# A graph kernel's attention weights written to PSUM as well, and its one-hots made by four scalar comparisons

## What is computed

```python
Q, K, V = x @ WQ, x @ WK, x @ WV             # per node, in 8 heads
Eh = edge_attr @ WE                          # per edge
score = exp(clip((K[src] * Q[dst] / sqrt(16) * Eh).sum(-1), -5, 5))   # per edge and head
wV = segment_sum(V[src] * score, dst)        # per node
Z = segment_sum(score, dst)
h = x + wV / (Z + 1e-6)                      # then a batch norm over the nodes
```

## Time and profile before

| | |
|---|---|
| timed runs | 5692.21, 5694.81, 5681.8 us; median 5692.21 |
| the profiled execution | span of 4693.0 us from its first to its last instruction; no other time of it is given |
| TensorE busy | 3812.3 us (81%) |
| VectorE busy | 3158.1 us (67%) |
| GpSimd busy | 3369.7 us (72%) |
| ScalarE busy | 1078.1 us (23%) |
| layer 0's loop over chunks | 145.7 to 2300.0 us |
| layer 0's gathers | 81.1 to 2286.1 us, 1661 of them |
| layer 1's gathers | 2443.8 to 4538.9 us, 1661 of them |

### The profile page before, as it was taken

The page is one execution under the profiler, slowest core; times in us unless marked ns, Lnnn a source line. Parts: engine busy times, 40 slices in busy tenths (PEclk is TensorE's granted clock), DMA queues, the critical chain, the costliest instruction groups (busy, mean ns, idle before and its releaser), DMA issues. The chain is left out here.

```text
span 4693.0 us, 76906 instructions
## 1 busy us (share of the span) xinstructions
PE 3812.3 (81%) x19332; PEld 3161.6 (67%) x19333; DVE 3158.1 (67%) x8279; ACT 1078.1 (23%) x4010; POOL 3369.7 (72%) x3437
## 2 busy tenths in 40 slices
PE   6889899989989988888898977777777777777778
PEld 5777777777778877767567755655555556555555
DVE  1877677677777776777646866666666666666657
ACT  3100010000000000000034433333333333333324
POOL 3677777777777777777557777777777777777752
PEclk9887787787776787888687555555555555555559
DMA  7666665666666666666424322222222222222224
GB/s 279 182 182 184 176 189 176 179 183 181 183 181 182 182 183 174 185 179 183 148 86 97 61 61 61 61 61 61 61 61 61 61 61 60 60 61 61 61 58 154
DMA packets 376029, 593.47 MB, mean 126 GB/s; under 512 B 151298, under 2 KB 204520, under 8 KB 374488
## 3 DMA queue, kind: packets, MB, share of 16 engines
q0 software_dynamic: 132880, 330.18, 27.4%
q1 hardware_dynamic: 241544, 255.24, 18.2%
q10 hardware_dynamic: 1552, 7.43, 0.4%
HBM read 551.16 MB, written 40.54 MB: 126 GB/s over the span
## 5 line engine op out<-in xcount | busy, mean ns | idle before, releaser
L393 POOL DMA_INDIRECT kv_g<-kv_table,idx x1661 | 1678.2, 1010 | 568.0 <-issue 498.7
L1065 POOL DMA_INDIRECT xg<-xl_table,idx x1661 | 1583.0, 953 | 519.3 <-issue 498.6
L1130 PEld LDWEIGHTS ps_sum<-pw,xg 128*128 128x128 f32 x3328 | 740.9, 328 | 165.9 <-DVE pws L1271 165.5
L1130 PE MATMUL ps_sum<-pw,xg 128*128 128x64 f32 x3328 | 819.1, 428 | 4.7 <-DVE pws L1271 2.2
L452 PE MATMUL ps_sum<-kv_g,hot 128*64 128x136 f32 x3328 | 606.6, 339 | 246.8 <-issue 245.8
L1117 PE MATMUL ps_tops<-ident,top 128*64 128x128 f32 x832 | 285.9, 447 | 518.7 <-DVE top L1243 518.4
L452 PEld LDWEIGHTS ps_sum<-kv_g,hot 128*64 128x64 f32 x3328 | 480.9, 167 | 314.9 <-issue 310.2
L438 PE MATMUL ps_pair<-w,eat 128*128 128x128 f32 x3328 | 616.3, 342 | 5.1 <-issue 5.1
L438 PEld LDWEIGHTS ps_pair<-w,eat 128*128 128x128 f32 x3328 | 524.2, 240 | 109.3 <-issue 71.7
L442 PE MATMUL ps_pair<-qw,hott 64*128 64x128 f32 x3328 | 583.9, 326 | 2.9 <-DMA qw<-q_table 2.9
L1229 DVE SCALAR_TENSOR_TENSOR ps_lg<-raw 128x256 f32<-128x256 f32 x416 | 185.3, 445 | 573.4 <-ACT raw L1178 566.7
(11 more groups left out here) (160 smaller groups left out, 4684.9 us busy)
## 6 DMA issues: line engine op xcount, KB each, us to landing
eat<-in_edges SPq DMA_DIRECT2D x416, 256.0 KB
local<-local_table SPq DMA_DIRECT2D x416, 128.0 KB, 3.8
kv_g<-kv_table,idx POOLq DMA_INDIRECT x1661
xg<-xl_table,idx POOLq DMA_INDIRECT x1661
qw<-q_table SPq DMA_DIRECT2D x416, 32.0 KB
adw<-ad_row SPq DMA_DIRECT2D x416, 32.0 KB, 5.1
kv_table<-kv_out SPq DMA_DIRECT2D x25, 512.0 KB, 2.6
xl_table<-xl SPq DMA_DIRECT2D x25, 264.0 KB, 2.8
```

The costliest lines, as they stand in the source:

```text
L393: nc.gpsimd.indirect_dma_start(out=kv[:, u, k, 0:2 * D], out_offset=None, in_=m["kv_table"], in_offset=bass.IndirectOffsetOnAxis(ap=idx[:, ...
L1065: nc.gpsimd.indirect_dma_start(out=xg[:, u, k], out_offset=None, in_=m["xl_table"], in_offset=bass.IndirectOffsetOnAxis(ap=idx[:, u // B, ...
L1130: nc.tensor.matmul(ps_sum[:, b, 0:W], xg[:, u, k, 0:D], pw[:, b, k], start=(k == 0), stop=(k == K - 1))
```

## The change

The PSUM bank that held the numbers 0 to 63 now holds the attention weights. ScalarE computes Exp of the scores twice, once into `kv_g` as before and once into this bank, and raises the semaphore `weighed` with the second. `value` reads the weights from the bank. `one_hot` no longer has the copy of the numbers in PSUM; it makes the one-hot slot by slot, with four `tensor_scalar` instructions that compare `m["iota"]` in SBUF (128 x 64) with one node number per partition. The copy of the numbers to PSUM ahead of the loop goes.

```diff
-        ps_iota = ps("ps_iota", [P, CE])[:, 0:W]
+        ps_weights = ps("ps_weights", [P, CE])[:, 0:K * H].rearrange("p (k h) -> p k h", h=H)
...
             def weigh(c, u):
                 act.wait_ge(scored, c + 1)
-                nc.scalar.activation(kv[:, u, :, 2 * D:ROW0], score[:, u % 2].rearrange("p (k h) -> p k h", h=H),
-                                     ACT.Exp).then_inc(weighed, 1)
+                scores = score[:, u % 2].rearrange("p (k h) -> p k h", h=H)
+                nc.scalar.activation(kv[:, u, :, 2 * D:ROW0], scores, ACT.Exp)
+                nc.scalar.activation(ps_weights, scores, ACT.Exp).then_inc(weighed, 1)
...
-            do(nc.vector.tensor_copy(ps_iota, m["iota"][:]))
...
             def one_hot(c, u):
-                nc.vector.tensor_tensor(hot[:, u % 4],
-                                        m["dst_local"][:, bass.ds(c, 1), :].rearrange("p a k -> p (a k)")
-                                        .unsqueeze(2).to_broadcast([P, K, W]),
-                                        ps_iota.unsqueeze(1).to_broadcast([P, K, W]),
-                                        ALU.is_equal).then_inc(hot_ready, 1)
+                slots = m["dst_local"][:, bass.ds(c, 1), :].rearrange("p a k -> p (a k)")
+                for k in range(K):
+                    last = nc.vector.tensor_scalar(hot[:, u % 4, k], m["iota"][:], slots[:, k:k + 1], None, ALU.is_equal)
+                last.then_inc(hot_ready, 1)
...
             def value(c, u):
                 dve.wait_ge(weighed, c + 1)
                 values = kv[:, u, :, D:2 * D].rearrange("p k (h d) -> p k h d", d=DH)
-                nc.vector.tensor_tensor(values, values, kv[:, u, :, 2 * D:ROW0].unsqueeze(3).to_broadcast([P, K, H, DH]),
+                nc.vector.tensor_tensor(values, values, ps_weights.unsqueeze(3).to_broadcast([P, K, H, DH]),
                                         ALU.mult).then_inc(valued, 1)
```

## The result

| | before | after |
|---|---|---|
| median of timed runs | 5687.01 us (5678.54 to 5694.81, 4 runs) | 5734.22 us (5727.5 to 5736.32, 4 runs) |
| profiled execution, span | 4693.0 | 5725.5 |

The ratio is 1.009, with a 95% interval of 1.0071 to 1.0109: the changed kernel is 47 us slower. The prediction said 78 us faster, with a range of its own that ended at 5662 and one over rivals A and B that ended at 5694.

The account below looks back on a forecast made before the run. GpSimd's queue of gathers was taken to bound layer 0's loop. Product -103, comparisons' cost to gathers +17 and tie +8 gave -78 us, so 5692.2 - 78 = 5614 us; own range 5578 to 5662, over rivals A and B to 5694.

Parts of the forecast that it names:

- A: Layer 0's gathers wait for the whole train of four comparisons: gain 31 us, 5661 us; chance 0.13.
- Rival B: Nothing to be seen: timed runs bound elsewhere in layer 0's stage, say by TensorE at 1.2 GHz; 5692 us; chance 0.10.
- I take 78 off the median: Final step: the gain summed for the profiled execution, 78 us, taken off the timed median 5692.2, giving 5614 us.
- the 999.2 us: Timed median above the profiled span, placed by no view; gain 78, 58 or 94 us by the way it is read.
- rival D: Slower, VectorE the bound in layer 0: fast chunk 4.62 us, 46 us slower, 5738 us; chance 0.06.
- C: Slower: the comparisons hold off layer 0's gathers in place of V's product, 31 us slower, 5723 us; chance 0.09.
- V's product, -103 us: Layer 0: with weights read from PSUM, gathers no longer stand behind the product; at most 103 us given back.
- The comparisons: Layer 0's one-hots: 0.20 us per comparison, VectorE +0.22 us a chunk, gathers delayed 17 us, bounds 4 and 64.
- The stretch of 0.1 us a chunk: Layer 0: VectorE's estimated stretching beside gathers, part of a fast chunk going from 3.97 to 4.30 us.
- The second Exp, 0 us: ScalarE in layer 0: 0.23 us at most, covered by 0.4 us of VectorE work, so cost nothing.
- The tie, 8 us: Layer 0: gathers need 5.03 us a chunk, TensorE and VectorE allow 5.05; 8 us more, between 0 and 30.
- Layer 1 unchanged: Layer 1 is not touched by the change and was expected to stay unchanged.

Follow-up runs that it names:

- before_fourth: The kernel before, unchanged, profiled once more on chip 1, where before took 5683.3 us: 5690.61 us.
- hot_only_b: The kernel before with only the one-hots made by four scalar comparisons, on chip 1: 5732.87 us, ratio 1.0078.
- v_only_c: The kernel before with only V's product from PSUM and the second Exp, old one-hot kept, on chip 8: 5766.17 us, ratio 1.0035.
- v_only: The kernel before with only V's product from PSUM and the second Exp, old one-hot kept, on chip 3: 4618.3 us, ratio 0.9825.
- v_only_b: The kernel before with only V's product from PSUM and the second Exp, old one-hot kept, on chip 0: 4622.49 us, ratio 0.9815.
- after_again: The changed kernel again, on chip 0, where the kernel before took 4711.51 us: 4627.75 us, ratio 0.9825.
- more_exp: The kernel before with a second Exp on ScalarE into a spare tile, ahead of the signal weighed, on chip 7: 5745.05 us, ratio 1.0001.
- act_signal: The kernel before with layer 0's gathers waiting for ScalarE's copy of the sums, not TensorE's signal, on chip 1: 5733.05 us, ratio 1.0084.

## Why the prediction was wrong

- **The bound.** "GpSimd's queue is the bound of layer 0's loop" holds for the execution that was profiled and for chips with 4700. In the timed runs it doesn't: GpSimd is busy 1356.55 of 2140 us (`before_fourth`) and waits for TensorE.
- **The step that failed** is "I take 78 off the median", with the 999.2 us treated as something that is added, or that scales the gain. All three ways considered (a constant, a slower pitch, everything slower by 1.21) keep the gathers as the bound. Rival B named the fourth, another bound in this stage, and put 603 of the 999 us there; it was given 0.10 with the argument that the rest would stay unexplained. The runs place 476 of the 999 us in this loop and 420 in the other. What bounds there is, as far as the runs show it, neither TensorE's clock alone nor GpSimd's pitch but the chain from the sum over its copy and the turned sums to the next gathers, with TensorE's signals held between the links.
- **The sign.** Once the gathers are not the bound, shortening them gives nothing, and what is left of the change is its cost: that of the comparisons on VectorE for the most part, by `hot_only_b`, and by `v_only_c` perhaps 20 us of the other half. Rival B stopped at no change. It needed rival D's term too: D had VectorE's time as what counts, for another reason (a chunk of 4.62 us), and that its 5738, and C's 5723, lie near the 5734 measured is luck: the fast chunk is 4.18 us and no gather waits for a train. B and D's term together would have been a forecast of slower. The +0.9% is close to `hot_only_b`'s +0.78%.
- **V's product, -103 us.** The mechanism is right on chips with 4700, the size was too large: `v_only` gave 83 us and `v_only_b` 89, with a gathers' mean of 959 ns in both. The rest is what the turned one-hot L554 holds once the product doesn't (above), a term that the prediction put at nothing. With the change the mean is 960 (956 forecast). In after it is 975, and that gave nothing.
- **The comparisons.** One takes 277 ns, not 200, and its shortest, 238, is above the bound of 220 that was drawn from L547. Four take 0.78 us of VectorE (326.3 us over 416 chunks), where the prediction had 0.62, less than four times 0.277 since they overlap. The stretch of 0.1 us a chunk that was added for gathers is in that already: the fast chunk at 2.4 GHz went from 3.94 to 4.18 us, not to 4.30. The cost to the gathers, 17 us with bounds of 4 and 64, was 7.4 to 8.7 us by my count (some 22 in after). Rivals A and C are out: `after_again`'s longest gather is 1.25 us.
- **The second Exp, 0 us.** Right: VectorE waits 0.8 us for it in all (L575), and `more_exp` is 1.0001.
- **The tie, 8 us, and the total.** -78 forecast, -84 measured on chip 0, with a span of 4621.6 against 4615. That they agree so well is in part luck: the product gave 14 to 20 us less than its term, and the comparisons, with the tie, cost 5 (`after_again` against `v_only_b`) and not 25. The granted clock, taken as constant, rose from 0.79 to 0.84 in the windows, which by the prediction's own quotient for TensorE and VectorE takes the tie away.
- **Layer 1 unchanged.** Right: its loop is 2449.4 in after and 2450.0 in `before_fourth`.

What stays open: what holds TensorE's signals on chips 1, 7 and 8; and why `v_only_c` (+20 us) and `act_signal` (+48 us) are slower there, though neither adds VectorE time. The second is as large as the whole loss of the result. So it isn't shown that the loss is VectorE's time alone: an edit may also cost by how it shifts a chunk against the held signals, though `more_exp` adds to ScalarE's part of the chunk and costs nothing. `v_only_c` has the further wait for the one-hot, which no run tests. `act_signal` makes the gathers wait for one link more of the held chain, 483 us for ScalarE (L499), less than the 539 us of `before_fourth`. Its difference lies in layer 0 (a loop of 2675.6 us against 2630.6). For `v_only_c` there is no trace of before on its chip; its loop takes 2668.2 us, that of `more_exp` on chip 7 2651.0.

## What to carry to other kernels

Compare the profiled span with the timed median before anything else. If they differ by more than the runs scatter, the profile shows another balance of bounds than the one that is timed, and each term of the sum needs a price in both: what it gives if the bound seen is the bound, and what is left of it if it isn't. An edit that trades a little of one engine's time for relief of another wins in the first and loses in the second.

## What the runs showed of the hardware

- The same kernel takes 4701 to 4712 us on two chips and 5683 to 5747 on three, with signals of TensorE that arrive up to several microseconds late while GpSimd issues bursts of indirect DMAs (4.6 us in the stretch shown). With two gathers in a burst and not four the kernel took 793 us less, and no sum signal of layer 0 was late (116 were in `v_only_c` on the same chip).
- A product of 128x512 with one input in SBUF and one in PSUM takes 670 ns, as with both in SBUF (674). Of 200 gathers beside it alone none was over 12 ns late; with both inputs in SBUF, 298 were, by 103 us together.
- A gather that started within a scalar operation of VectorE over 64x512 (0.47 us, input and output in SBUF) took longer by up to 0.29 us, the more the longer the operation still ran; one that started before it wasn't held by it. All 172 late gathers of `after_again` met a scalar operation.
- A comparison of 128x64 with a scalar per partition takes 238 to 500 ns, 277 in the mean; four in a row take 0.78 us.
- In the profiled pair with few gathers the granted TensorE clock fell from 0.89 to 0.77 with the change, whose VectorE chunk is some 0.25 us longer, and a chunk took 0.64 us more (layer 0's loop 2180.0 against 1912.5 us, over 415 chunks). By the ratio of the timed runs it is 186 us, about 0.45 us a chunk. An edit's cost there was more than its own time; that the clock follows from the edit isn't shown.
